# Cross-attention of a fused two-layer kernel: key tiles weighed in blocks of 12, one block later, in place of 6, two blocks later

## The reference

```python
q, k, v = heads(LN(x) @ W_Q + b_Q), heads(ctx @ W_K + b_K), heads(ctx @ W_V + b_V)   # 16 heads of 32
scores = einsum('bhqd,bhkd->bhqk', q, k) / sqrt(32)      # 512 queries x 8192 keys a head
attn = softmax(scores, axis=-1)
x = x + merge(einsum('bhqk,bhkd->bhqd', attn, v)) @ W_O + b_O
```

## Time and profile before

| | |
|---|---|
| median of 3 runs | 3908.72 us (3897.31 to 3910.78) |
| the profiled execution's own time | 3904.15 us |
| its span | 3902.8 us |
| mean granted clock of TensorE over the span | 0.954 |
| busy over the span | PE 93%, DVE 65%, ACT 49%, POOL 46% |
| matmuls in records | 17868 |
| DVE maxima, line 636 | 2048, 1290.4 us busy |
| ACT exps, line 745 | 1024, 1019.3 us busy |
| POOL additions, lines 759 and 762 | 342 and 310, 818.6 and 737.3 us busy |

### The profile page before, as it was taken

The page is one execution under the profiler, slowest core; times in us unless marked ns, Lnnn a source line. Parts: engine busy times, 40 slices in busy tenths (PEclk is TensorE's granted clock), DMA queues, the critical chain, the costliest instruction groups (busy, mean ns, idle before and its releaser), DMA issues. The chain is left out here.

```text
span 3902.8 us, 46028 instructions
## 1 busy us (share of the span) xinstructions
PE 3611.3 (93%) x17868; PEld 2318.5 (59%) x17868; DVE 2529.3 (65%) x3462; ACT 1920.9 (49%) x1962; POOL 1776.0 (46%) x744
## 2 busy tenths in 40 slices
PE   6999899989999999986797999999999887799997
PEld 5777688755555555432674455555554375588886
DVE  2222234347777777637796877777776464699997
ACT  2111211145555555642683456555656321577785
POOL 1111111149999999920000599999998320100000
PEclk8999999999999999996897799999999998799999
DMA  6455655553333333102686233333331101799996
GB/s 254 162 185 186 204 174 174 180 154 87 87 74 85 87 87 82 51 23 106 263 356 215 56 85 87 87 85 81 88 87 30 49 1 48 276 370 373 376 380 252
DMA packets 215944, 593.83 MB, mean 152 GB/s; under 512 B 42624, under 2 KB 108192, under 8 KB 161840
## 3 DMA queue, kind: packets, MB, share of 16 engines
q1 hardware_dynamic: 176944, 517.47, 40.8%
q10 hardware_dynamic: 36864, 67.13, 4.6%
q0 software_dynamic: 1920, 6.29, 0.5%
HBM read 470.64 MB, written 120.09 MB: 151 GB/s over the span
## 5 line engine op out<-in xcount | busy, mean ns | idle before, releaser
L636 DVE TENSOR_REDUCE maxima<-psum 128x1 f32<-128x512 f32 x2048 | 1290.4, 682 | 387.7 <-PE psum L631 384.1
L745 ACT ACTIVATE pt<-psum 128x1024 f32<-128x1024 f32 x1024 | 1019.3, 1025 | 702.9 <-PE psum L656 697.7
L759 POOL TENSOR_TENSOR exp_sums<-pt 128x1024 f32<-128x1024 f32 x342 | 818.6, 2394 | 266.0 <-PE psum L672 132.8
L631 PE MATMUL psum<-ks,first_q 96*128 96x512 f32 x2048 | 814.5, 447 | 19.7 <-DMA first_q<-q_parts 8.4
L762 POOL TENSOR_TENSOR exp_sums<-exp_sums,pt 128x1024 f32<-128x1024 f32 x310 | 737.3, 2378 | 45.8 <-ACT pt L745 1.5
L668 PE MATMUL psum<-pt,vs 128*32 128x512 f32 x4096 | 675.5, 599 | 4.6 <-DVE head_rows L772 2.2
L631 PEld LDWEIGHTS psum<-ks,first_q 96*128 96x128 f32 x2048 | 394.0, 192 | 477.7 <-DVE maxima L636 321.2
L672 PE MATMUL psum<-exp_sums,constants 128*32 128x512 f32 x1408 | 671.3, 599 | 0.0
L656 PE MATMUL psum<-qs,ks 97*128 97x512 f32 x2048 | 649.8, 400 | 15.1 <-ACT pt L745 15.1
L1422 DVE TENSOR_TENSOR moe_cut<-moe_raw,moe_cut 128x2048 fp32r<-128x2048 f32 x244 | 557.1, 2291 | 57.7 <-ACT moe_cut L1364 52.7
L1364 ACT CAST moe_cut<-moe_raw 128x2048 fp32r<-128x2048 f32 x244 | 467.2, 1921 | 64.9 <-PE psum L97 64.9
(11 more groups left out here) (310 smaller groups left out, 4395.9 us busy)
## 6 DMA issues: line engine op xcount, KB each, us to landing
moe_raw<-in_moe_w SPq DMA_DIRECT2D x244, 1024.0 KB, 7.8
ks<-k_parts SPq DMA_DIRECT2D x384, 256.0 KB, 4.6
k_parts<-kparts ACTq DMA_DIRECT2D x256, 256.0 KB, 2.9
cx<-in_ctx SPq DMA_DIRECT2D x32, 1024.0 KB
v_heads<-vrow SPq DMA_DIRECT2D x32, 1024.0 KB, 5.8
vs<-v_heads SPq DMA_DIRECT2D x32, 1024.0 KB, 5.3
first_q<-q_parts SPq DMA_DIRECT2D x96, 64.0 KB, 4.0
qs<-q_parts SPq DMA_DIRECT2D x96, 64.0 KB, 4.9
```

What stands on the lines that cost most here:

```text
L631: pe.matmul(self.c.bank[self.FIRST_BANK + k % 3], self.first_q[s][:, t * P:(t + 1) * P], self.ks[s][part][0:3 * DH, at:at + CHUNK], start= ...
L636: dve.tensor_reduce(self.maxima[:, h % 2, i % TT, i // TT:i // TT + 1], self.c.bank[self.FIRST_BANK + k % 3], X, ALU.max).then_inc(*self.f ...
L745: act.activation(self.pt[:, self.slot(h, b) + i:self.slot(h, b) + i + 2, :], self.c.psum[:, at:at + 2, :], ACT.Exp).then_inc(*self.exp.up())
L759: engine.tensor_tensor(to, self.pt[:, slot:slot + R, :], self.pt[:, slot + R:slot + 2 * R, :], ALU.add).then_inc(*signal.up())
```

## The change

A block has up to 12 tiles: five of 12 and one of four a head. It is weighed one block later, in `rounds(b)` rounds: four, and two for the last. The number of additions stays two per full block and one in the last, over as many tiles as there are rounds (2048 columns, and 1024 in the last). The ring of exponentials grows from 18 to 24 tiles, that of the sums from 2 x 2 to 2 x 4. The rows of ones of head 0 are written in blocks 1 to 4.

```diff
-    ROUNDS, LAG = 2, 2
-    BLOCK = 3 * ROUNDS
-    BLOCKS = [list(range(t, min(t + 3 * 2, KT))) for t in range(0, KT, 3 * 2)]
+    BLOCK, LAG = 12, 1
+    BLOCKS = [list(range(t, min(t + 12, KT))) for t in range(0, KT, 12)]
...
-    ONES = (2, 4, 6, 8)
+    ONES = (1, 2, 3, 4)
...
+    def rounds(self, b):
+
+        return -(-len(self.BLOCKS[b]) // 3)
+
     def adds(self, b):
 
-        return -(-len(self.BLOCKS[b]) // self.ROUNDS) - 1
+        return -(-len(self.BLOCKS[b]) // self.rounds(b)) - 1
...
-            self.sums = c.sb(st, f"exp_sums{l}", [P, 2, self.ROUNDS, TOK])
+            self.sums = c.sb(st, f"exp_sums{l}", [P, 2, self.BLOCK // 3, TOK])
...
-            for r in range(self.ROUNDS):
+            for r in range(self.rounds(b)):
...
-                if r < len(tiles):
-                    item = self.sums[:, sums, r, :] if self.adds(b) else pt[:, slot + r, :]
-                    last = pe.matmul(bank[self.OUT_BANK][3 * DH:4 * DH, :], c.ones[:, 0:DH], item, start=b == 0 and r == 0, stop=b == NB - 1 and r == min(self.ROUNDS, len(tiles)) - 1)
+                last = pe.matmul(bank[self.OUT_BANK][3 * DH:4 * DH, :], c.ones[:, 0:DH], self.sums[:, sums, r, :], start=b == 0 and r == 0, stop=b == NB - 1 and r == self.rounds(b) - 1)
...
-        tiles, g, slot, R = self.BLOCKS[b], h * len(self.BLOCKS) + b, self.slot(h, b), self.ROUNDS
+        tiles, g, slot, R = self.BLOCKS[b], h * len(self.BLOCKS) + b, self.slot(h, b), self.rounds(b)
...
-        to = self.sums[:, g % 2]
+        to = self.sums[:, g % 2, 0:R, :]
```

## The result

The change makes the kernel slower: 4029.51 us in the median (4028.39 to 4037.67), against 3909.75 before, a ratio of 1.0317 (95% interval 1.0303 to 1.0331). The forecast was 4006 in a range of 3950 to 4060, with slower at 0.91.

The account below looks back on a forecast made before the run. TensorE, busy 93%, was taken as the bound, with VectorE's reads pacing the new stretch. Terms of -0.6, +2.15, -0.36, +0.8 and +1.0 gave +3.0 us a head, 50 a layer, 100 for both: 4006 us, range 3950 to 4060.

Parts of the forecast that it names:

- Weighing: Weights-by-values passes after a block's scores: one four-round weighing 3.55 us against 3.66 for two two-round ones, -0.6 us a head.
- The stretch of 12: Score matmuls of a 12-tile block: VectorE's reads set the pace, 6.70 us against 2 x 3.13, +2.15 us a head.
- The fold: Block folding the previous head: excess falls from 0.77 to 0.4 us, first weighing no longer waiting, -0.36 us a head.
- The hold: VectorE's negated maxima, held until GpSimd's addition ends: next read delayed 1.45 us in a paced stretch, +0.8 us a head.
- The wait at the short block: TensorE at the weighing behind a head's four-tile last block waits for GpSimd's second addition: +1.0 us a head.
- GpSimd's addition: One addition over 2048 columns on GpSimd: taken as 4.65 us, between 4.62 and 4.76.
- much slower: Rival: additions over 5 us or a hold of a whole addition, 4100 to 4110 us; lower clock ends here too; chance 0.09.
- 4.1 us of wait in each of heads 14 and 15: Layer's last heads: TensorE waits for GpSimd's additions, against some 0.5 now; +7 us, head 14's first blocks +1.
- faster: Rival: matmul shape changes cost and VectorE follows, TensorE alone setting the stretch; -88 us, 3816 us; chance 0.04.
- at most 34 us on five weighings fewer a head: Within the faster rival: at most 0.1 us each side of a weighing, 34 us for 32 heads, about 3870 us.

Follow-up runs that it names:

- e1: Changed kernel with each of VectorE's maximum reads taken over 256 of the 512 columns (half reads): 3956.4 us, 1.0117 of before.
- e11: Kernel before with blocks of six weighed in pairs, narrow additions kept, and the maxima negated by ScalarE: 3936.8 us, 1.0079 of before.
- e10: Kernel before with maxima negated by ScalarE and the previous head folded one pair of tiles earlier: 3892.8 us, 0.9964 of before.
- e4: Changed kernel with the maxima negated by ScalarE instead of VectorE: 4024.9 us, 1.0299 of before.
- e3: Changed kernel without GpSimd's second addition in the fifth block: 4010.0 us, 1.0261 of before.
- e5: Changed kernel with maxima negated by ScalarE and without GpSimd's second addition in the fifth block: 3935.0 us, 1.0076 of before.
- e7: Changed kernel with half reads by VectorE and without GpSimd's second addition in the fifth block: 3942.3 us, 1.0086 of before.
- e8: Kernel before with blocks of six weighed in pairs, GpSimd's additions kept at 1024 columns: 4058.0 us, 1.0388 of before.

## Why the prediction was right, by its own steps

1. Weighing: 3.57 us against 3.55 forecast. The short one was misread: the weighings before take 1.85 to 1.86 us, not "1.83 in most blocks", so a pair is 3.70 and the gain 0.13 us, 0.65 a head.
2. The stretch of 12: 6.70 to 6.72 against 6.70. Right, and the cause is shown, by e1 (5.83 with half reads) and by e11 (6.70 with narrow additions).
3. The fold: the block is 10.69 against 10.28, an excess of 0.41 as forecast. The reason given for the gain was wrong. It wasn't that the first weighing no longer waits for the rows (e10). TensorE's 0.81 us of fold lay open before; now part of them lie where TensorE would wait for VectorE anyway. With half reads the excess is 6.73 - 5.83 = 0.9 again.
4. The hold: the stretch is 7.93 against 8.15, so the term is +0.6, not +0.8. The negation took 0.84 us (0.86 in the median) where 1.1 was expected, since GpSimd's second addition ends at 4.3 us of the block and not at 4.5. The size was near; what I missed is how a stop there goes with the clock.
5. The wait at the short block: 3.22 - 2.08 = 1.14 us against 1.0. Items 4 and 5 were added as two costs, which is right for the sum, but they are not independent: e4.
6. GpSimd's addition: 4.59 us in the mean against the 4.65 taken.

A head without a spell is 58.1 against 58.06 forecast; in part the errors of items 1, 2, 4 and 5 cancel, and each is under 0.25 us. The sum fell 24 us short of the measured change, and this is where: fourteen head distances of a layer grew by 45.5 us (45.1 in layer 1), not 42, of which 43 are the heads without a spell and the rest spells of the lower clock; the end of a layer, from the last column maximum to the first transpose of the output, by 12.2 and 12.3 us, not 8 (64.2 to 76.4), also at a lower clock (0.92 from 1650 to 1780 us, where it was 1.00 before); the starts of the two attention stages by about 4 together. Another 6 us lie between the attentions, in stages that the change doesn't touch; among the runs that stretch took 422 to 428 us, and its cause stays open. So the main term left at nothing was the granted clock, which the forecast named only as a way into the rival "much slower". At the layers' ends no run parts it from the waits. The forecast had 4.1 us of wait in each of heads 14 and 15; the trace shows it in one only:

```profile
1708.12 1.07 PE L671 MATMUL psum<-pt,vs 128*32 128x512 f32 x3 [3.96 <-POOL exp_sums L763]
...
1765.65 0.63 PE L671 MATMUL psum<-pt,vs 128*32 128x512 f32 x3 [0.84 <-POOL exp_sums L763]
```

In head 15 GpSimd's additions end 13.9 us into the block, as forecast (14.1), but TensorE comes there at 13.2, not 10: its stretch of the block takes 5.76 us and the weighing behind it 6.21 in place of 3.57, at the lower clock.

The rival "faster" fell where it was said to: a read every 0.47 us isn't there. That the long weighings are cheaper is real (3.57 against 3.70) but small. The Trainium skill, TensorEngine Tiling (Array Packing), section Tiling Modes, says that changing the tiling mode drains TensorE; from the rows the forecast put at most 34 us on five weighings fewer a head. The measured gain of a weighing is 0.13 us for each pair, some 21 us over 32 heads.

## What to carry to other kernels

A block length sets how much one engine can fall behind another before the pause in which it catches up: here VectorE, busy 62% on average, sets the pace, since its queue is three banks deep. So cost a new block length by the slow engine's run within the block, not by shares. And before grouping work more coarsely, look at which small operations share something with the long ones: a 0.17 us negation took up to 2.4 us behind an addition, and moving it to ScalarE was worth 17 us in the kernel before and 75 in the one after once its other wait was gone (e3 to e5): some 29 of the 75 by the hold itself (57.0 to 55.94 us a head), the rest by the spells that went with it.

## What the runs showed of the hardware

- The negation (VectorE, TENSOR_SCALAR over 128 x 4 elements from SBUF to SBUF), 0.17 us when GpSimd is idle, ends 0.02 to 0.03 us after GpSimd's running addition, whatever is left of that: 0.84, 1.70, 1.94 and 2.39 us in four kernels. The column maximum (TENSOR_REDUCE, 128 x 64 to 128 x 4, SBUF to SBUF) isn't held: 0.22 us beside the same additions. Nor are VectorE's reads from PSUM, which run on at 0.60 to 0.61 us, nor the negation on ScalarE (0.20 us).
- The granted clock fell to its lower level after TensorE had stood in the middle of a stretch: after stops of 0.83 to 0.88 us in nine of 28 heads (the kernel after) or in nearly all (e3), after stops of 1.9 us in nearly all (e1, e7, e8). It didn't fall in such stretches without the stop (e5, e11: 1.00). After TensorE had stood 2.0 us before the weighing behind a short block it fell in head 0 of each layer and in none of heads 1 to 13 (e4). What tells these cases apart I can't say from these runs.
- A spell of the lower clock can be partly hidden: in the head at 1342 us the fifth block took 13.1 us instead of 11.5, but the short stretch behind it 2.07 instead of 3.22, since GpSimd, which keeps its pace, had caught up.
